# Beta moved onto the diagonal of the decay scan, sums of squares as two rounded products split by GpSimd, and the output sums placed between the halves of the key projection, in a decoder layer with a gated delta net

## The reference

```
qkv = x @ W_qkv.T ; z = x @ W_z.T ; beta = sigmoid(x @ W_b.T)
decay = exp(-softplus(x @ W_a.T + dt_bias) * exp(A_log))
qkv = causal depthwise convolution of qkv, 4 taps
k   = k / max(|k|, 1e-12)
per token: Sk = k . state ; delta = (v - Sk) * beta
           state = state * decay + k (x) delta ; o = q . state
out = rmsnorm(o) * norm_w * silu(z) ; y = out @ W_out.T
```

## Time and profile before

| | |
|---|---|
| median of 3 runs | 4566.03 us (4562.16 to 4568.08) |
| the profiled execution, its span | 4563.68 us, 4561.9 us |
| busy over the span: TensorE, VectorE, ScalarE, GpSimd | 4014.6, 3163.8, 2239.2, 1893.7 us |
| delta net's sections | from about 134 to 3,060 us |
| cross-attention, feed-forward | from about 3,100 us, from about 4,100 us |

### The profile page before, as it was taken

The page is one execution under the profiler, slowest core; times in us unless marked ns, Lnnn a source line. Parts: engine busy times, 40 slices in busy tenths (PEclk is TensorE's granted clock), DMA queues, the critical chain, the costliest instruction groups (busy, mean ns, idle before and its releaser), DMA issues. The chain is left out here.

```text
span 4561.9 us, 75168 instructions
## 1 busy us (share of the span) xinstructions
PE 4014.6 (88%) x26288; PEld 2924.0 (64%) x26288; DVE 3163.8 (69%) x5082; ACT 2239.2 (49%) x4061; POOL 1893.7 (42%) x1852
## 2 busy tenths in 40 slices
PE   3899999999999999999999999985788879389998
PEld 2677777677777776777767677762344444168887
DVE  3788888888888888888888888874555556532222
ACT  1565656565655556565656565652444445321111
POOL 1364545554554546454555455542233332411110
PEclk8899999999999999999999999996899989689999
DMA  2001010101010101101010101103444553000001
GB/s 74 15 29 35 27 34 20 41 24 32 30 36 25 36 20 32 33 26 35 20 41 24 32 29 34 26 15 69 78 84 77 85 83 59 38 23 19 19 14 37
DMA packets 134066, 172.39 MB, mean 38 GB/s; under 512 B 12524, under 2 KB 79980, under 8 KB 133132
## 3 DMA queue, kind: packets, MB, share of 16 engines
q1 hardware_dynamic: 131212, 166.03, 15.5%
q10 hardware_dynamic: 2432, 1.05, 0.1%
HBM read 143.12 MB, written 21.76 MB: 36 GB/s over the span
## 5 line engine op out<-in xcount | busy, mean ns | idle before, releaser
L405 PE MATMUL pj<-xh,w_hi 128*128 128x512 f32 x1536 | 686.4, 447 | 25.4 <-ACT conv_k L612 16.7
L990 POOL TENSOR_TENSOR silu_z<-silu_z,exp_z 128x512 f32<-128x512 f32 x128 | 184.6, 1442 | 1212.7 <-ACT exp_z L629 1212.7
L405 PE MATMUL pj<-xh,w_lo 128*128 128x512 f32 x1536 | 607.5, 395 | 0.0
L405 PE MATMUL pj<-xl,w_hi 128*128 128x512 f32 x1536 | 602.9, 392 | 0.0
L1510 DVE TENSOR_REDUCE row_max<-s 128x1 f32<-128x512 f32 x512 | 342.0, 685 | 264.4 <-PE s L1264 260.7
L975 POOL TENSOR_SCALAR b_t<-qk_masked,beta_section 128x256 f32<-128x256 f32 (+1 forms) x512 | 490.7, 967 | 20.2 <-ACT qk_masked L714 19.6
L1444 ACT ACTIVATE probs<-s 128x512 f32<-128x512 f32 x512 | 290.6, 595 | 335.8 <-PE s L1288 267.5
L756 DVE SCALAR_TENSOR_TENSOR conv_v<-conv_in,conv_w_section,conv_v 128x512 f32<-128x512 f32 x384 | 402.0, 1047 | 19.4 <-ACT conv_v L612 5.5
L680 ACT ACTIVATE kk_masked<-tp 128x512 f16<-128x512 f32 x320 | 191.3, 598 | 321.8 <-PE tp L496 318.2
L405 PEld LDWEIGHTS pj<-xh,w_hi 128*128 128x128 f32 x1536 | 291.9, 190 | 81.0 <-issue 28.9
L405 PEld LDWEIGHTS pj<-xh,w_lo 128*128 128x128 f32 x1536 | 289.7, 189 | 67.3
(11 more groups left out here) (259 smaller groups left out, 10258.9 us busy)
## 6 DMA issues: line engine op xcount, KB each, us to landing
w_raw<-in_w_in SPq DMA_DIRECT2D x128, 256.0 KB, 3.4
decays<-decay_by_head SPq DMA_DIRECT2D x64, 512.0 KB, 3.8
decays<-decay_by_head SPq DMA_DIRECT2D x64, 256.0 KB, 4.9
q_stack<-qk_parts SPq DMA_DIRECT2D x128, 128.0 KB
k_stack<-qk_parts SPq DMA_DIRECT2D x128, 128.0 KB
f_raw<-in_f_w SPq DMA_DIRECT2D x32, 256.0 KB, 2.6
x_all<-in_x SPq DMA_DIRECT2D x4, 1024.0 KB, 11.2
source<-in_ctx SPq DMA_DIRECT2D x8, 512.0 KB
```

What stands on the lines that cost most here:

```text
L405: mm = pe.matmul(pj[j % 2][:, :], a[:, j, k * P:(k + 1) * P], b[:, k, bp * WIN:(bp + 1) * WIN], start=(n == 0), stop=(n == 3 * KT - 1))
```

## The change

Beta comes into the decay scan: `beta_diag` holds beta on the diagonal where `scan_diag` held ones, so that `dec` is the decay product times beta. GpSimd fills it for the next section, in two instructions. `dve_a` is then a product of `dec` and the key products, read from PSUM for both value heads at once, four instructions instead of eight; it moves to the tail of the section before, between the scans. The key products are no longer copied to SBUF by ScalarE, and the inverse's tile that shared their room gets one of its own. `pool_b` becomes two broad products. The key-key products are issued ahead of the second chunk's `d0p`, and the halves of the last gate projection move one group later.

Each sum of squares becomes two products of rounded tiles with a rounded matrix of ones. GpSimd rounds the squares and takes the rest: for the keys at the end of its section, behind the weight splits, for the output at its start, behind `silu_z` and ahead of `pool_b`. On TensorE the first output sum stands behind the first half of the key projection, the second behind the second half.

At the start one load (`scan_diag`) falls away, and `gates` runs in a block of its own that gives its semaphores back.

```diff
-        kk = m.sb("kk_masked", [P, 2, TRI])
-        qk = m.sb("qk_masked", [P, 2, TRI])
+        qk = m.sb("query_products", [P, 2, TRI])
+        tu0 = m.sb("t_and_u0", [P, 2 * NM * P], F16)
+        beta_diag = m.sb("beta_diag", [P, NM, TRI + 2])
         dec = m.sb("decays", [P, NM, TRI + 2])
...
+        sq_lo = m.sb("square_lo", [P, WIN], F32R)
+        ksq_hi, osq_hi, osq_lo = res, [u_f[:, p, :] for p in range(PV)], [sq_lo, v_r]
...
         def pe_norms(pe, t):
-            E["ksq"].wait(pe, t, 0)
-            pe.matmul(ms[0][:, :], ones, ksq[:, :], start=True, stop=True).then_inc(E["kssp"].sem, 1)
+            E["klo"].wait(pe, t, 0)
+            pe.matmul(ms[0][:, :], ones_r, ksq_hi[:, :], start=True, stop=False)
+            pe.matmul(ms[0][:, :], ones_r, sq_lo[:, :], start=False, stop=True)\
+                .then_inc(E["kssp"].sem, 1)
+        kq_bank = (ms[0], ms[1], up, ms[0])
         def pe_kq(pe, t, i):
             if i == 0:
                 E["kn"].wait(pe, t, 0)
+            if i == 2:
                 E["cv"].wait(pe, t, QUERY * 3 + 2)
             if i == 3:
-                E["km"].wait(pe, t, 0)
-            bank = (ms[0], ms[1], up, ms[0])[i]
-            right, o = (kn, cv[QUERY])[i % 2], (i // 2) * SEQ
+                E["at"].wait(pe, t, 1)
+            bank, right, o = kq_bank[i], (kn, cv[QUERY])[i // 2], (i % 2) * SEQ
             pe.matmul(bank[:, 0:SEQ], kn[:, o:o + P], right[:, o:o + SEQ], start=True, stop=False,
                       skip_group_check=True)
             pe.matmul(bank[:, SEQ:TRI], kn[:, o + P:o + SEQ], right[:, o + P:o + SEQ], start=False, stop=True,
         def pe_out_norms(pe, s, p, more):
-            E["osq"].wait(pe, s, p)
+            E["olo"].wait(pe, s, p)
             if more:
-                E["km"].wait(pe, s + 1, 3)
-            pe.matmul(ms[p][:, :], ones, osq[p][:, :], start=True, stop=True).then_inc(E["oss"].sem, 1)
+                E["at"].wait(pe, s + 1, 3)
+                E["km"].wait(pe, s + 1, 1)
+            pe.matmul(ms[p][:, :], ones_r, osq_hi[p], start=True, stop=False)
+            pe.matmul(ms[p][:, :], ones_r, osq_lo[p][:, :], start=False, stop=True)\
+                .then_inc(E["oss"].sem, 1)
...
             pe_values(pe, s, 0)
             pe_values(pe, s, 1)
+            proj(KEY, 0)
             if prev:
                 pe_out_norms(pe, s + -1, 0, True)
+            pe_first(pe, s, 0, prev)
+            proj(KEY, 1)
+            if prev:
                 pe_out_norms(pe, s + -1, 1, True)
-            proj(KEY, 0)
-            pe_first(pe, s, 0, prev)
             pe_first(pe, s, 1, prev)
-            proj(KEY, 1)
...
-            proj(GATE + 1, 0)
-            E["rhs1r"].wait(pe, s, 0)
             E["uc"].wait(pe, s, 1)
-            pe_group(pe, xp[0], lambda q: u_f[:, 1, mat(q)], v_r, "d0p")
-            proj(GATE + 1, 1)
-            E["d0"].wait(pe, s, 1)
-            pe_group(pe, xp[1], lambda q: a_t[:, q, SEQ:TRI], d0[:, :].bitcast(F32), "rp")
             if nxt:
                 pe_kq(pe, s + 1, 0)
                 pe_kq(pe, s + 1, 1)
+            E["rhs1r"].wait(pe, s, 0)
+            pe_group(pe, xp[0], lambda q: u_f[:, 1, mat(q)], v_r, "d0p")
+            proj(GATE + 1, 0)
+            E["d0"].wait(pe, s, 1)
+            pe_group(pe, xp[1], lambda q: a_t[:, q, SEQ:TRI], d0[:, :].bitcast(F32), "rp")
+            proj(GATE + 1, 1)
             E["res"].wait(pe, s, 1)
             pe_group(pe, tp, lambda q: u_f[:, 1, mat(q)], res, "dp2")
             if nxt:
                 pe_kq(pe, s + 1, 2)
                 pe_kq(pe, s + 1, 3)
             E["delta"].wait(pe, s, 1)
-            E["bt"].wait(pe, s, 3)
+            E["bt"].wait(pe, s, 1)
...
-                act_kq(act, s + 1, 0)
-                act_kq(act, s + 1, 1)
-                act_kq(act, s + 1, 2)
-                act_kq(act, s + 1, 3)
+                act_queries(act, s + 1, 0)
+                act_queries(act, s + 1, 1)
             act_sigmoid(act, s, 1)
-        def act_kq(act, t, i):
-            E["kq"].wait(act, t, i)
-            act.activation((kk, qk)[i % 2][:, i // 2, :], (ms[0], ms[1], up, ms[0])[i][:, 0:TRI], ACT.Copy)\
-                .then_inc(E["km"].sem, 1)
+        def act_queries(act, t, b):
+            E["kq"].wait(act, t, 2 + b)
+            E["bt"].wait_before(act, t)
+            act.activation(qk[:, b, :], kq_bank[2 + b][:, 0:TRI], ACT.Copy).then_inc(E["km"].sem, 1)
...
-            dve.tensor_tensor_scan(dec[:, i, :], dec[:, i, :], diag, 0.0, ALU.mult, ALU.add).then_inc(E["dec"].sem, 1)
-
-        def dve_a(dve, s):
-
-            E["km"].wait(dve, s, 3)
-            E["beta_s"].wait(dve, s, 0)
-            for q in range(NM):
-                E["dec"].wait(dve, s, q)
-                for c, sl in enumerate((slice(0, SEQ), slice(SEQ, TRI))):
-                    before = dec[:, slot(q), sl.start + c:sl.stop + c]
-                    dve.scalar_tensor_tensor(out=a_t[:, q, sl], in0=kk[:, q // PV, sl],
-                                             scalar=beta_s[:, 2 * (q // PV) + c, q % PV:q % PV + 1], in1=before,
-                                             op0=ALU.mult, op1=ALU.mult).then_inc(E["at"].sem, 1)
-            E["at"].wait(dve, s, 7)
+            dve.tensor_tensor_scan(dec[:, i, :], dec[:, i, :], beta_diag[:, i, :], 0.0, ALU.mult, ALU.add).then_inc(E["dec"].sem, 1)
+        def dve_a(dve, t, b, c):
+            E["kq"].wait(dve, t, b)
+            E["dec"].wait(dve, t, b * PV + PV - 1)
+            sl = (slice(0, SEQ), slice(SEQ, TRI))[c]
+            by_head = dec[:, b:NM:2, sl.start + c:sl.stop + c]
+            dve.tensor_tensor(a_t[:, b * PV:(b + 1) * PV, sl], by_head,
+                              kq_bank[b][:, sl].unsqueeze(1).to_broadcast([P, PV, sl.stop - sl.start]), ALU.mult)\
+               .then_inc(E["at"].sem, 1)
+        def dve_inverse(dve, s):
+            E["at"].wait(dve, s, 3)
...
-            dve_beta(dve, s, bp, hk)
-            dve_a(dve, s)
+            dve_inverse(dve, s)
...
-            dve_gate(dve, s, 0)
             if nxt:
                 dve_decays(dve, t, 1)
+            dve_gate(dve, s, 0)
             dve_rest(dve, s, 1)
             if nxt:
+                dve_a(dve, t, 0, 0)
+            dve_residual(dve, s, 1)
+            if nxt:
+                dve_a(dve, t, 0, 1)
                 dve_decays(dve, t, 2)
-            dve_residual(dve, s, 1)
+            E["dp2"].wait(dve, s, 1)
+            dve.tensor_tensor(delta[1], tp[:, :], d0[:, :].bitcast(F32), ALU.add).then_inc(E["delta"].sem, 1)
             dve_gate(dve, s, 1)
             if nxt:
                 dve_decays(dve, t, 3)
-            E["dp2"].wait(dve, s, 1)
-            dve.tensor_tensor(delta[1], tp[:, :], d0[:, :].bitcast(F32), ALU.add).then_inc(E["delta"].sem, 1)
+                dve_a(dve, t, 1, 0)
+                dve_a(dve, t, 1, 1)
...
-        def pool_b(pool, s, q):
-            E["km"].wait(pool, s, q // PV * 2 + 1)
-            E["beta_s"].wait(pool, s, 0)
+        def pool_beta(pool, t, hk, bp):
+            if t:
+                E["dec"].wait(pool, t - 1, NM - 1)
+            for c in range(2):
+                o = c * (SEQ + 1) + 1
+                by_head = beta[:, 4 * bp + c:4 * bp + 4:2, hk * PV:(hk + 1) * PV].rearrange("p b h -> p h b")
+                pool.tensor_tensor(beta_diag[:, :, o:o + P].rearrange("p (h b) t -> p h b t", b=2),
+                                   ident.unsqueeze(1).unsqueeze(1).to_broadcast([P, PV, 2, P]),
+                                   by_head.unsqueeze(3).to_broadcast([P, PV, 2, P]), ALU.mult)\
+                    .then_inc(E["bd"].sem, 1)
...
+        def pool_b(pool, s):
+            E["km"].wait(pool, s, 1)
+            E["dec"].wait(pool, s, NM - 1)
             if s:
                 E["op"].wait(pool, s - 1, PV - 1)
+            by_head = dec[:, :, :].rearrange("p (h b) t -> p b h t", b=2)
+            of = b_t[:, :, :].rearrange("p (b h) t -> p b h t", b=2)
             for c, sl in enumerate((slice(0, SEQ), slice(SEQ, TRI))):
-                pool.tensor_scalar(b_t[:, q, sl], qk[:, q // PV, sl], beta_s[:, 2 * (q // PV) + c, q % PV:q % PV + 1],
-                                   None, ALU.mult).then_inc(E["bq"].sem, 1)
-            E["dec"].wait(pool, s, q)
-            E["bq"].wait(pool, s, 2 * q + 1)
-            pool.tensor_tensor(b_t[:, q, 0:SEQ], b_t[:, q, 0:SEQ], dec[:, slot(q), 1:SEQ + 1], ALU.mult)\
-                .then_inc(E["bt0"].sem, 1)
-            pool.tensor_tensor(b_t[:, q, SEQ:], b_t[:, q, SEQ:], dec[:, slot(q), SEQ + 2:], ALU.mult).then_inc(E["bt"].sem, 1)
+                pool.tensor_tensor(of[:, :, :, sl], qk[:, :, sl].unsqueeze(2).to_broadcast([P, 2, PV, sl.stop - sl.start]),
+                                   by_head[:, :, :, sl.start + c + 1:sl.stop + c + 1], ALU.mult).then_inc(E["bt"].sem, 1)
...
+        def pool_key_squares(pool, t):
+            E["ksq"].wait(pool, t, 0)
+            if t > 1:
+                E["oss"].wait(pool, t - 2, 0)
```

(30 more changed lines are left out.)

53 lines of the change are left out of this document (26 added, 27 removed).

## The result

The changed kernel takes 4,962 us (median of four runs, 4,956 to 4,963), the kernel before 4,567 beside it: 1.0865 times as long, interval 1.0846 to 1.0884. I forecast 4,810, with 4,640 to 4,900 as range. The direction and the place were right; the size, 395 us in place of 246, lies outside the range.

What follows compares the result with a forecast made beforehand. The stage was taken as bound by turns between TensorE and VectorE. Per section 4.1 - 0.8 - 0.27 = +3.0, 191 us in 63 sections, plus 51 for key norms and 4 for ends: 246, giving 4,810 us; range 4,640 to 4,900.

Steps and rivals of the forecast that it cites:

- the late key norm: Head's first section: key squares queue behind GpSimd's output weights split, so TensorE's key norm comes 3.4 us later, 15 times: 51 us.
- levels: The six levels after the first x_l: key and query convolutions, freed from b_t products, give back 0.8 us a section.
- tail: Section's end: key norm 0.43 us shorter, less a 0.16 stall for the right side: -0.27 us a section.
- weight splits of third sections: GpSimd's split of the next head's weights ends before the key squares come, as the loads are earlier.
- the clock: TensorE's granted clock over the stage, forecast to stay unchanged at full.
- The new head: Section start: GpSimd's squares, norms and blocked gating products put the first x_l at T+12.0 for T+7.92, +4.1 us.
- The turns: VectorE and GpSimd alternate at two-input SBUF work: head +4.1 us, chance 0.48; without them +2.15, 4,690 us, chance 0.24.
- (b): Rival: every turn on the SBUF ports goes against VectorE, 4.6 us a section, 4,930 us; chance 0.13.
- (c): Rival: squares hidden and TensorE sets the pace, so shorter norms win 76 us, 4,490 us; chance 0.11.

Runs made afterwards that it cites:

- e2: Changed kernel with GpSimd's two beta diagonals for the next section moved behind the rest of the gated output: 4,852 us.
- e5: Changed kernel with unsplit fp32 sums of squares, output sums back directly behind the value transposes, beta diagonals behind the gated output's rest: 4,539 us, 0.9935 of before.
- e10: e5 with the next head's weight loads held until the third section's first value convolution is through: 4,519 us, 0.9901 of before.
- e6: Changed kernel with dummy products, read by nobody, filling TensorE's waits: 4,924 us.
- e7: e5 with squares rounded by ScalarE, each sum one rounded product, the lower part left out: 4,562 us, 0.9988 of before.
- e1: Changed kernel with sums of squares as before, one fp32 product each, nothing of them on GpSimd; the change's places on TensorE kept: 4,779 us.

## Why the prediction fell short

The head and the late key norm came as forecast. What failed are two terms of the sum that were mis-sized, levels (-0.8) and tail (-0.27), and two that it put at nothing, the weight splits of third sections and the clock ("unchanged at full").

**The new head**: the mechanism was right, and the sum too: T+12.0 for `x_l` was forecast and measured, in all four kinds of section to 0.2 us. 63 x 4.1 = 258 us. That it agrees to a tenth is luck, as its links don't. The squares, norms and exponentials run 0.3 to 0.6 us later than I had them. I let `b_t` block the first gating product, which took 0.68 unblocked, so that the second ended at T+11.15 and not 11.8. And the 16-wide copy of the weights, to which I gave 0.2 us, took 1.01. The turns, which I gave 0.48 against 0.24 for their absence, are shown by e2 (1.7 us in the head) and e5 (1.5 us).

**The late key norm**: right, 3.46 us for 3.4.

**Levels**: -0.8 us forecast, +0.1 measured (first `x_l` to key norm 21.56 us in a second section before, 21.65 after). Key and query convolutions did lose their `b_t` neighbours, and the key's takes 2.33 for 2.77. But I had the subtractions of the gated output meet a convolution "still". They now meet the query's, 4.15 us in place of 2.67, and not the first value's, 2.31 for 3.77. VectorE in the second section shown above:

```profile
1679.01 4.15 DVE L758 SCALAR_TENSOR_TENSOR conv_q<-conv_in,conv_w_section,conv_q 128x512 f32<-128x512 f32 x3
...
1683.75 2.31 DVE L758 SCALAR_TENSOR_TENSOR conv_v<-conv_in,conv_w_section,conv_v 128x512 f32<-128x512 f32 x3
```

The value's place has slack behind it (in e2 that convolution grows by 0.8 us and the key norm comes no later), the query's has none, so what one gives back the other takes. **Tail**: -0.27 forecast, +0.1 measured. The key norm did become shorter, but the `rp` group behind it now waits 0.17 us for ScalarE's copy of `delta_first`, a wait that the longer sum had covered. Both together are 1.27 us in 63 sections, 80 us of the missing 149.

**Third sections**: I had said that the earlier loads let the splits end before the key squares come. They do, but they lie on both value convolutions: the first split starts at T+19.9 in place of T+22.0, and the late head has moved these convolutions from T+16.2 and T+21.1 to T+21.0 and T+26.7. VectorE in the changed kernel's third section, query and both values:

```profile
1728.57 4.16 DVE L758 SCALAR_TENSOR_TENSOR conv_q<-conv_in,conv_w_section,conv_q 128x512 f32<-128x512 f32 x3
...
1733.31 4.50 DVE L758 SCALAR_TENSOR_TENSOR conv_v<-conv_in,conv_w_section,conv_v 128x512 f32<-128x512 f32 x3
...
1739.00 3.91 DVE L758 SCALAR_TENSOR_TENSOR conv_v<-conv_in,conv_w_section,conv_v 128x512 f32<-128x512 f32 x3
```

beside GpSimd's splits, the first and the last:

```profile
1733.28 1.28 POOL L978 TENSOR_TENSOR w_lo<-w_raw,w_hi 128x512 fp32r<-128x512 f32 x1
...
1740.75 1.61 POOL L978 TENSOR_TENSOR w_lo<-w_raw,w_hi 128x512 fp32r<-128x512 f32 x1
```

The query's 4.16 is that of a second section too. The two values take 8.4 us where a changed second section has 2.31 + 2.32 = 4.6. An undisturbed third section takes 52.5 us, a second 49.6, where the difference was 1 us: some 2 us, 30 us over 15 sections. e10 shows the cause for the side of the loads: with the splits 4.1 us later an undisturbed third section falls from 46.2 to 44.9 us.

**The clock**: "granted clock unchanged at full" was wrong. It falls to half in 314 us of the stage, 24 before; e6 prices it at 40 to 50 us. This was no case among my rivals at all, although the profile of the kernel before showed a clock of 0.85 from 3,100 to 4,100 us, where TensorE was busy 75%. The missing terms make 80 + 30 + 45 = 155 us for the missing 149; the clock's is an estimate to 10 us, and first sections may hold some of it twice.

**The rivals**: the blocked-everywhere case (b) at 4,930 came nearest in time, for another reason. The other side (c) needed the squares hidden and TensorE as the bound in the head. e7 takes the squares off GpSimd altogether, and nothing was won from shorter sums.

Open: how much of the first sections' 9.1 us is the clock's (4.4 lie ahead of `x_l`, 3.4 between it and the key norm, 1.3 behind; e6's fillers take 1.6 off), and why a head's fourth section has a tail 1 us longer than its second, before and after alike.

## What to carry over

When work is moved to an engine with time to spare, ask what it stands behind there and what waits for it: what the change touched on GpSimd fell from 14 to 12 us a section, and still the squares in it cost 183 us (e1), because four of its instructions came to lie between the output's squares and their norms, and two more, behind the weight splits, between the keys' and theirs. An instruction whose result is wanted late should not stand ahead of another engine's urgent work on the same memory side: moving two such instructions gave 106 to 110 us. And take TensorE's clock into the sum wherever a change opens waits in a stage that was nearly closed, here from 93 to 84% busy.

## What the runs showed of the hardware

- VectorE and GpSimd take turns on SBUF for whole instructions: the gating product took 0.68 us alone and 1.53 beside a GpSimd product of 1.49, and even a copy of 16 columns per partition took 1.01 us for 0.17. Products with one operand in PSUM did not: the one at 1671.05 took its 0.75 us beside `b_t`, and an addition at 1738.40 took 0.67 beside a weight split, 0.69 with GpSimd idle. The Trainium skill ("SBUF — State Buffer", two separate sides) calls it an exclusive lock, which e2 bears out.
- Less work on TensorE can be slower: e7 removes 56 us of its busy time and takes 23 us longer, with 126 us in place of 72 at the half clock; e6 adds useless products in waits and takes 38 us less, with 72 us in place of 314. That the clock is the whole cause in e7 is likely and not shown.
- A product of 1,024 columns on GpSimd with one operand broadcast and one of 512 took 3.32 us together, less than the 3.8 that I had worked out from the width.
